# Values' products of four steps in one block of TensorE's queue, four banks for the exponentials, and one product of the first attention moved from GpSimd to ScalarE

## What is computed

```python
# 1. attention of 16 heads of 16 columns in bf16, over a reshaped qkv
xs = conv3(x); xs = xs + xs @ pe_w.T
q, k, v = split(xs @ qkv_w.T).astype(bfloat16)
attn = softmax(q @ k.T / sqrt(16)); o = attn @ v
x = layernorm(x + o @ out_w.T)
# 2. in fp32, 16 heads: masked self attention plus attention over the context
y  = softmax(causal(q @ k.T * scale)) @ v        # 512 x 512 scores, 4 tiles of keys
y += softmax(qc @ kc.T * scale) @ vc             # 512 x 1024 scores, 8 tiles of keys
x = layernorm(x + y @ Wp + bp)
# 3. routed feed forward: argmax over 8 clusters, then over 8 tiles, a small table per token
x = layernorm(x + ffn(x))
```

## Time and profile before

| | us |
|---|---|
| median of three runs | 3291.19 |
| the profiled execution | 3298.75 |
| its span, first to last instruction | 3296.8 |
| TensorE matmul busy | 2772.2 (84%) |
| VectorE busy | 1921.9 (58%) |
| ScalarE busy | 1342.1 (41%) |
| GpSimd busy | 386.0 (12%) |
| mean granted TensorE clock | 0.820 of full speed |

### The profile page before, as it was taken

One profiled execution on the slowest core, in us unless ns is written; L12 is line 12 of the kernel. 1 busy time (PEld: TensorE's weight loads), 2 busy tenths in 40 slices (PEclk: granted clock), 3 DMA queues, 4 the chain that ended last, 5 costly groups with the idle time before them and its releaser, 6 DMA issues.

```text
span 3296.8 us, 46102 instructions
## 1 busy us (share of the span) xinstructions
PE 2772.2 (84%) x12994; PEld 1096.7 (33%) x12994; DVE 1921.9 (58%) x5166; ACT 1342.1 (41%) x2880; POOL 386.0 (12%) x473
## 2 busy tenths in 40 slices
PE   6899858997689977899778997789977899688995
PEld 1343313433134331443314433144331433324322
DVE  7576275753857538564385743856438564486633
ACT  3345243452524525255252552525525154262541
POOL 3100121001200003000030000300003000130000
PEclk7899858999589975899758997589975899758986
DMA  5300032000410004100051000510005000050000
GB/s 133 59 1 1 1 77 52 1 1 1 93 36 1 1 1 100 29 1 1 0 102 28 1 1 0 104 25 1 1 1 109 20 1 1 1 115 1 1 1 7
DMA packets 284202, 91.83 MB, mean 28 GB/s; under 512 B 269344, under 2 KB 279712, under 8 KB 283936
## 3 DMA queue, kind: packets, MB, share of 16 engines
q1 hardware_dynamic: 283936, 88.60, 13.3%
HBM read 17.27 MB, written 4.19 MB: 7 GB/s over the span
## 4 chain that ended last, share of the span: by engine, by line
PE 69%; DVE 14%; ACT 6%; issue 5%; DMA 3%; POOL 2%; DVEq 0%; POOLq 0%; SPq 0%; ACTq 0%
PE bank L1090 16%; PE bank L908 13%; PE bank L1106 11%; PE bank L1056 9%; PE bank L1086 6%; DVE work L592 5%; PE bank L1052 4%; DMA work<-work 3%; ACT work L497 3%; PE bank L1010 2%; ACT work L462 1%; POOL work L426 1%; PE bank L1002 1%; PE bank L1067 1%; PE bank L1114 1%
## 5 line engine op out<-in xcount | busy, mean ns | idle before, releaser
L497 ACT ACTIVATE work<-bank 128x512 f32<-128x512 f32 (+3 forms) x1536 | 754.2, 544 | 892.9 <-PE bank L1090 603.8
L1090 PE MATMUL bank<-q_c,k_c 32*128 32x512 f32 x2048 | 731.7, 669 | 61.8 <-ACT work L497 61.8
L690 DVE TENSOR_REDUCE top_half<-bank 128x1 f32<-128x512 f32 x1024 | 635.4, 683 | 192.9 <-PE bank L1056 192.6
L1056 PE MATMUL bank<-k_c,q_c 32*128 32x512 f32 x2048 | 499.9, 635 | 6.1 <-DVE top_half L690 6.1
L462 ACT ACTIVATE work<-work,neg 128x512 bf16<-128x512 bf16 x512 | 362.8, 709 | 236.9 <-DVE work L592 126.0
L948 PE MATMUL bank<-k,q 32*128 32x512 bf16 x512 | 280.1, 609 | 180.4 <-DVE work L592 145.1
L1106 PE MATMUL bank<-work,v_flat 128*32 128x512 f32 (+3 forms) x3072 | 385.8, 580 | 0.0
L1090 PEld LDWEIGHTS bank<-q_c,k_c 32*128 32x128 f32 x2048 | 226.4, 193 | 357.7 <-ACT work L497 265.4
L592 DVE TENSOR_SCALAR_CACHE_REDUCE work<-bank 128x512 bf16<-128x512 f32 x512 | 321.5, 680 | 34.5 <-issue 31.5
L686 DVE CUSTOM_DVE_ANT_0 masked<-bank,mask_w 128x384 bf16<-128x384 f32 (+3 forms) x512 | 231.3, 489 | 146.3 <-PE bank L1052 141.9
L1086 PE MATMUL bank<-q_s,k_s 32*128 32x512 f32 (+3 forms) x1024 | 268.3, 500 | 19.1 <-ACT work L497 16.7
(11 more groups left out here) (172 smaller groups left out, 2370.9 us busy)
## 6 DMA issues: line engine op xcount, KB each, us to landing
xT_pad<-xT SPq DMA_DIRECT2D x16, 256.0 KB, 4.2
ctx_sb<-ctxT SPq DMA_DIRECT2D x8, 512.0 KB, 3.3
x_res<-x SPq DMA_DIRECT2D x8, 512.0 KB, 5.1
out<-y_sb SPq DMA_DIRECT2D x8, 512.0 KB, 4.5
work<-work SPq DMA_TRANSPOSE x128, 4.3
qk_sb<-qkT SPq DMA_DIRECT2D x1, 512.0 KB, 4.9
...
```

What stands on the lines that cost most here:

```text
L497: nc.scalar.activation(pT[:, k % PT_SLOTS, g, q0:S], bank[:, RING + n % EXP_RING, 0:S - q0], ACT.Exp, scale=SCALE).then_inc(pT_ready, 1)
L690: nc.vector.tensor_reduce(top_half[:, g, t, half:half + 1], scores, AX.X, ALU.max, negate=True).then_inc(slot_out, 1)
L1056: mm(dst, q_c[rows, i, P * t:P * (t + 1)], k_c[rows, i, S * half:S * (half + 1)], start=True, stop=True, tile_position=(GW * g, 0)).then_i ...
L1090: mm(dst, k_c[rows, i, P * t:P * (t + 1)], q_c[rows, i, :], start=True, stop=True, tile_position=(GW * g, 0)).then_inc(sT_mm, 1)
```

## The change

Three things change.

- **The values' products** of four steps are issued together (`BURST`), after the scores of steps 4, 8 and, for the last four steps of a group, step 0 of the next group or the end of the loop. Each such block writes a slot of VectorE's ring of banks 0 to 3, not bank 7. VectorE copies it out of PSUM (`outputs`): the block of self attention and the first of cross attention as a plain copy, the second of cross attention by adding to what was copied. ScalarE's `o_copy` is gone. pT has six slots of a step.
- **Bank 7** goes to the exponentials: `EXP_RING` is 4, in the loop and for the projections (`unit`), and unit 3 waits for the values that stood in bank 7.
- **The first attention**: ScalarE multiplies the fourth tile of every head, after the exponentials of the next head, with an activation Copy with a scale per row. GpSimd does none. VectorE does three tiles of head 15 too. e1 and p1T have four slots.

The lines that only rename semaphores or lay out the slots in `work` are left out:

```diff
     ALL_STEPS = HG * STEPS
-    RING, EXP_RING = 4, 3
+    RING, EXP_RING = 4, 4
+    BURST = 4
+    BURSTS = STEPS // BURST
...
-    A1_BANKS, E1_SLOTS = 6, 3
-    USES = ALL_SCORES + 4 * HG + EXTRAS
+    A1_BANKS, E1_SLOTS = 6, 4
+    USES = ALL_SCORES + (4 + BURSTS) * HG + EXTRAS
     UNITS, CTX_UNITS = 3 * HG, 2 * HG
-    PT_SLOTS = 4
+    PT_SLOTS = 6
...
                     order += [("max", m) for m in range(score_of(i, u, 0), score_of(i, u + 1, 0)) if m < ALL_SCORES]
+                    if burst_at(i, u):
+                        order.append(("pv",) + burst_at(i, u))
                     if u == 3:
...
                                   9: [("qk", 2), ("qk", 3)], 10: [("v", 0), ("v", 1)]}.get(u, [])
-            order.append(("o", CROSS, HG - 1))
+            order += [("pv", HG - 1, BURSTS - 1), ("o", CROSS, HG - 1)]
             assert len(order) == USES - (EXTRAS if last else 0)
...
+        def burst_at(i, u):
+            k = STEPS * i + u
+            return divmod(k // BURST - 1, BURSTS) if k % BURST == 0 and k > 0 else None
...
-                sp.wait_ge(p1_dve, b * P1_DVE + DVE_TILES * (h + 1) + (NT - DVE_TILES) * (h == H - 1))
+                sp.wait_ge(p1_dve, (b * H + h + 1) * DVE_TILES)
                 own_wait(nc.sync)
-                if h < H - 1:
-                    sp.wait_ge(p1_pool, (b * (H - 1) + h + 1) * (NT - DVE_TILES))
-                    own_wait(nc.sync)
+                sp.wait_ge(p1_act, (b * H + h + 1) * (NT - DVE_TILES))
+                own_wait(nc.sync)
                 if h >= E1_SLOTS:
...
-                def norm1(h):
-                    pool.wait_ge(rden_ready, b * H + h + 1)
-                    own_wait(nc.gpsimd)
-                    for t in range(DVE_TILES, NT):
-                        e = e1[:, h % E1_SLOTS, t, :]
-                        nc.gpsimd.tensor_scalar(e, e, rden1[:, h % 2, t:t + 1], None, ALU.mult).then_inc(p1_pool, 1)
-                for h in range(H - 1):
-                    norm1(h)
-                    if h == 11:
-                        pool.wait_ge(o1_copied, b * KD + 1)
-                        own_wait(nc.gpsimd)
-                        nc.gpsimd.tensor_copy(featA[:, 0, :].rearrange("p (r c) -> p r c", c=CHUNKS),
-                                              o1T[:, 0, :].rearrange("p (c r) -> p r c", c=CHUNKS)).then_inc(tok_ready, 1)
+                pool.wait_ge(o1_copied, b * KD + 1)
+                own_wait(nc.gpsimd)
+                nc.gpsimd.tensor_copy(featA[:, 0, :].rearrange("p (r c) -> p r c", c=CHUNKS),
+                                      o1T[:, 0, :].rearrange("p (c r) -> p r c", c=CHUNKS)).then_inc(tok_ready, 1)
                 rstd(0)
...
+                def norm1(h):
+                    act.wait_ge(rden_ready, b * H + h + 1)
+                    for t in range(DVE_TILES, NT):
+                        e = e1[:, h % E1_SLOTS, t, :]
+                        nc.scalar.activation(e, e, ACT.Copy, scale=rden1[:, h % 2, t:t + 1]).then_inc(p1_act, 1)
                 def out1(k):
...
                     if k >= PT_SLOTS:
-                        act.wait_ge(pv_done, b * ALL_STEPS + k - PT_SLOTS + 1)
+                        act.wait_ge(slot_in, base + uses[("pv",) + divmod((k - PT_SLOTS) // BURST, BURSTS)] + 1)
                     q0 = P * u if u < NT else 0
...
-                def o_copy(kind, i):
-                    act.wait_ge(pv_done, b * ALL_STEPS + STEPS * i + (NT if kind == SELF else STEPS))
-                    nc.scalar.copy(o_rows[:, kind, :], bank[:, 7, :]).then_inc(o_copied, 1)
                 for h in range(H):
                     exp1(h)
+                    if h >= 1:
+                        norm1(h - 1)
                     if h == 11:
                         out1(0)
+                norm1(H - 1)
                 context_keys()
...
                         probabilities(i, u)
-                        if u == 1 and i > 0:
-                            o_copy(CROSS, i - 1)
-                        if u == 5:
-                            o_copy(SELF, i)
-                o_copy(CROSS, HG - 1)
...
                     if h >= 2:
-                        dve.wait_ge(p1_pool, (b * (H - 1) + h - 1) * (NT - DVE_TILES))
+                        dve.wait_ge(p1_act, (b * H + h - 1) * (NT - DVE_TILES))
                     nc.vector.reciprocal(rden1[:, h % 2, :], denb1[:, h % 2, :]).then_inc(rden_ready, 1)
...
                     dve.wait_ge(rden_ready, b * H + h + 1)
-                    for t in range(DVE_TILES if h < H - 1 else NT):
+                    for t in range(DVE_TILES):
                         e = e1[:, h % E1_SLOTS, t, :]
...
                                             ALU.min).then_inc(cross_top, 1)
+                def outputs(i, q):
+                    use, n = uses["pv", i, q], BURSTS * i + q
+                    kind = SELF if q == 0 else CROSS
+                    dve.wait_ge(slot_in, base + use + 1)
+                    if q < 2:
+                        nc.vector.tensor_copy(o_rows[:, kind, :], slot(use)).then_inc(slot_out, 1)
+                    else:
+                        dve.wait_ge(slot_out, base + uses["pv", i, q - 1] + 1)
+                        nc.vector.tensor_tensor(o_rows[:, kind, :], slot(use), o_rows[:, kind, :], ALU.add).then_inc(slot_out, 1)
...
                                 maxima(score_of(i, u, g))
+                        if burst_at(i, u):
+                            outputs(*burst_at(i, u))
                         if u == 3 and i < HG - 1:
...
                                 first_v(base, uses)
+                outputs(HG - 1, BURSTS - 1)
                 finish(CROSS, HG - 1)
...
                     i, w = u // 3, unit_w[u % 3]
-                    if u >= 3:
-                        pe.wait_ge(pj_evac, b * UNITS + u - 2)
+                    if u >= EXP_RING:
+                        pe.wait_ge(pj_evac, b * UNITS + u - EXP_RING + 1)
+                    if u == 3:
+                        pe.wait_ge(vj_evac, (b + 1) * PAIRS)
                     project(bank[:, RING + u % EXP_RING, :], lambda k: w[:, k, P * i:P * (i + 1)], lambda k: featB[:, k, :]).then_inc(pj_mm, 1)
...
-                def pv(i, u):
-                    k = STEPS * i + u
-                    pe.wait_ge(pT_ready, b * ALL_SCORES + GH * (k + 1))
-                    if u < NT:
-                        pe.wait_ge(causal_done, b * HG * NT + NT * i + u + 1)
-                    if u == 0 and i > 0:
-                        pe.wait_ge(o_copied, b * 2 * HG + 2 * i)
-                    if u == NT:
-                        pe.wait_ge(o_copied, b * 2 * HG + 2 * i + 1)
-                    q0 = P * u if u < NT else 0
-                    for g in range(GH):
-                        at = u * H * (HD + 1) + (GH * i + g) * (HD + 1)
-                        last = mm(bank[GW * g:GW * (g + 1), 7, q0:S], v_flat[:, at:at + GW], pT[:, k % PT_SLOTS, g, q0:S],
-                                  start=(u in (0, NT)), stop=(u in (NT - 1, STEPS - 1)), tile_position=(0, GW * g))
-                    last.then_inc(pv_done, 1)
+                def pv(i, q):
+                    k = STEPS * i + BURST * q
+                    pe.wait_ge(pT_ready, b * ALL_SCORES + GH * (k + BURST))
+                    if q == 0:
+                        pe.wait_ge(causal_done, b * HG * NT + NT * (i + 1))
+                    dst = free_slot(base, uses["pv", i, q])
+                    for u in range(BURST * q, BURST * (q + 1)):
+                        q0 = P * u if u < NT else 0
+                        for g in range(GH):
+                            at = u * H * (HD + 1) + (GH * i + g) * (HD + 1)
+                            last = mm(dst[GW * g:GW * (g + 1), q0:S], v_flat[:, at:at + GW], pT[:, (STEPS * i + u) % PT_SLOTS, g, q0:S],
+                                      start=(u % BURST == 0), stop=(u % BURST == BURST - 1), tile_position=(0, GW * g))
+                    last.then_inc(slot_in, 1)
...
                 def o_transpose(kind, i):
-                    pe.wait_ge(o_copied, b * 2 * HG + 2 * i + kind + 1)
+                    pe.wait_ge(slot_out, base + uses["pv", i, 2 * kind] + 1)
                     dst = free_slot(base, uses["o", kind, i])
...
                             scoresT(i, u, g)
-                        if u > 1:
-                            pv(i, u - 2)
-                        elif i > 0:
-                            pv(i - 1, STEPS - 2 + u)
+                        if burst_at(i, u):
+                            pv(*burst_at(i, u))
                         if u == 3 and i < HG - 1:
...
                                 first_v(base, uses)
-                pv(HG - 1, STEPS - 2)
-                pv(HG - 1, STEPS - 1)
+                pv(HG - 1, BURSTS - 1)
                 o_transpose(CROSS, HG - 1)
```

11 lines of the change are left out of this document (5 added, 6 removed).

## The result

The changed kernel takes 2972.77 us (median of 4 runs, 2968.98 to 2974.19) against 3292.53 (4 runs, 3290.33 to 3295.98): a ratio of 0.9026, 95% interval 0.9011 to 0.9042.

A forecast was written before the change was run, and what follows sets the result against it. VectorE bounds the first attention, a chain through a bank on TensorE's queue the loop. Gains of 6.0 and 29.5 us a batch, less 6.0 friction, make 233 over eight; plus 20 for the clock, 253: 3038 us, range 2985 to 3185.

The forecast's parts named there:

- The signs that were named: Both stages: three tiles in 0.87, heads every 3.7; 32 product instructions in 3.6, VectorE's idle in one 3 us piece.
- Rival A: Main loop: VectorE takes over more than counted, maxima and TensorE wait behind late copies; time 3147; chance 0.2.
- B: Group 3 of the loop: the clock falls in all of it; time about 3240; chance 0.13.
- C: Groups 0 to 2: half clock where TensorE waits for VectorE's maxima, so slower; time 3351; chance 0.06.
- D: First attention: no gain, since ScalarE or TensorE is as slow as VectorE was; time 3086; chance 0.1.
- I take off 0.5 us for each of 12 blocks, 6.0: Main loop: friction, a block's hand-overs (a semaphore, a refill of two rings), deducted from each batch's gain of 35.1 us.
- The loop without friction: Main loop: gains by blocks of steps sum to 29.5 us a batch before any deduction for hand-overs.
- the terms for steps 1 to 4 of group 3: Group 3 without maxima: narrow tiles, block 2.3 and projection 3.7, written as 11.6 us against 15.8 before; gain 4.2.
- eight gains: Main loop: the gains of 1.6, 0.65 and 1, put at 7.1 us a batch, lost if VectorE takes over.
- The clock: Group 3, steps 5 to 8: half of the half-clock loss returns, 5 us in four of eight batches, 20 us.
- The term per head: First attention: without GpSimd's hold on VectorE a head takes 3.72 us, not 4.16; 14 x 0.43 = 6.0 us a batch.
- a wait that VectorE did not feel: First attention: the fourth slot ends the exponentials' wait for a slot, 0.88 us, said not to affect VectorE.

The follow-up runs named there:

- The copy done twice: Changed kernel with VectorE's copy of a block's sum done twice in each group's first two blocks, 64 copies of 0.69 us more: 2977.29 us, ratio 0.9070.
- one bank less: Changed kernel with three banks instead of four for the exponentials (EXP_RING 3), one bank unused: 3219.46 us, ratio 0.9781.
- blocks of one: Changed kernel with each step's products issued by themselves (BURST 1, 12 a group) instead of four steps' together: 2923.52 us, ratio 0.8905.
- blocks of two: Changed kernel with products issued two steps at a time (BURST 2, six a group) instead of four: 2977.09 us, ratio 0.9069.
- VectorE's four tiles: Kernel before the change with all four tiles of the first attention's products on VectorE, none on GpSimd, three slots: 3256.79 us, ratio 0.9903.

## Why the prediction was wrong

1. **Direction and mechanism: right.** The signs that were named are there: three tiles in 0.88, 32 instructions in 3.64, VectorE's idle time in one piece, steps 5 to 8 well below 15.5. Rival A did not happen: a copy ends 0.33 us before the first maximum. The copy done twice shows that this is all the cover there was. B and C did not happen in the changed kernel, and B did with one bank less. GpSimd is busy 192 us less (190 forecast). What the prediction does not divide is the loop's gain between its two causes: the bank carries it, and the blocks of four are not needed once the bank is there (by the runs with three banks and with blocks of one). D did not happen, though only just: ScalarE is busy 3.5 of a head's 3.65 us.

2. **The step that failed: "I take off 0.5 us for each of 12 blocks, 6.0".** The blocks took what the arithmetic without it said (13.8 for 13.9, 13.35 for 13.4, a mean of 12.5 for 12.5, and group 3 of batch 0, where the clock stood at 1.00, 43.7 for 43.7), and nothing is left over for 0.5 each. The terms that I summed were measured from the start of one operation to the start of another in the earlier trace rows (1.16 to the first maximum, 1.05 for the last tile), so the hand-overs were in them already, and I charged them twice: 48 us of the 77 between 253 and the profiled 330. What a further block does cost is 0.22 us by blocks of two, 0.2 of it in the products' own time. The same margin closed the range too early: the prediction had 2970 without friction and with the clock back, and took 2985 as the lower end; 2972.77 was measured.

3. **The loop without friction: right.** Fastest batch against fastest batch it went from 195.9 to 166.4, 29.5 us; the sum was 29.5 as well. The parts agree within 0.4 us each, but for one with 0.6, which is more than luck; that the sum agrees to the tenth is luck (the first steps of batch 0 took 0.8 us longer than those of the later batches, and the terms for steps 1 to 4 of group 3 add up to 11.4, not to the 11.6 that I wrote; the measured part is 11.8). In rival A, which speaks of eight gains, 7.1 is the sum of six. Windows of the loop in batches 1 and 7 of the kernel before, then batches 0, 1 and 7 of the changed kernel:

```profile
594.76:790.65 195.89, 185.06 (x1133) 70.78 (x1133) 105.29 (x226) 98.61 (x200) 10.26 (x16) 0.99 0.00 1
3032.30:3235.87 203.57, 191.41 (x1093) 66.40 (x1092) 90.56 (x204) 98.63 (x200) 10.17 (x16) 0.87 0.00 1
```

```profile
179.75:346.16 166.41, 161.96 (x1134) 79.77 (x1133) 111.86 (x238) 92.64 (x192) 10.59 (x16) 0.99 0.01 1
543.31:714.79 171.48, 167.02 (x1134) 80.86 (x1133) 111.78 (x238) 92.89 (x192) 10.59 (x16) 0.95 0.01 1
2751.50:2907.21 155.71, 151.61 (x1094) 68.58 (x1093) 96.85 (x216) 91.60 (x192) 10.16 (x16) 0.97 0.00 1
```

4. **The clock: 20 predicted, 30 by what is left** (265.7 less 8 x 29.5). It is not spread as I thought. In batches 0 to 6 the kernel before lost 42 us against its fastest batch and the changed one still loses 31, 5 in each of six batches; the last batch, which ran at 0.87 before and at 0.97 now, gave 18 more than its 29.5. The rows that I read of steps 5 to 8 of group 3 at 0.52 were one of several places, and the falls there did not go away: they became shorter and moved.

5. **Where the gain of the arithmetic was eaten within a batch:** in group 3. The parts there took 1.8, 2.5 and 1.5 us more than at full clock, and all 5.8 us are missing in batch 0, where the clock does not fall (group 3 takes 44.55 us for 50.36). So it is the clock. What brings it down is shown in part. Filling the gap ahead of step 6 kept the clock up behind it in all seven batches of the loop, and closing the gap of 2.2 us ahead of the last block did so for that block. But the first fall, around step 4, came with the gap before it filled, and batch 0 has all three gaps and no fall. So the last two gaps are a condition of the falls behind them, and not the only one; what else decides is open.

6. **First attention: 62 for 48.** The term per head was 0.43 and came as 0.51 (4.16 to 3.65). Two steps in it were off, though they moved the sum little: the fourth slot, which I called a wait that VectorE did not feel, is needed as soon as ScalarE has the product (4.03 a head without it; the whole gain hangs on it), and the Copy took 0.71, at the bound. 12.3 of the 62.4 us are none of the heads': in batches 1 to 7 the second head's scores start sooner, as in all kernels that ran with a changed program. VectorE at the turn of the batch, the kernel before and then the changed one:

```profile
452.82 0.69 DVE L592 TENSOR_SCALAR_CACHE_REDUCE work<-bank 128x512 bf16<-128x512 f32 x1 [5.38 <-issue]
```

```profile
407.12 0.69 DVE L588 TENSOR_SCALAR_CACHE_REDUCE work<-bank 128x512 bf16<-128x512 f32 x1 [3.33 <-issue]
```

Without these 12.3 us the stage gave 50. That this is near the 48 of the forecast is in part luck: from the second head's scores to the sums of head 15 it gave 59, 7.4 a batch where 6.0 was forecast, and what follows, which I took to keep its length, became 1.2 us a batch longer (39.5 for 38.3). In batch 3 the context's keys start 0.6 us later behind those sums, and a projection (`unit`) takes 3.06 us for 2.27, as it runs longer at the lower clock. Why the idle time at the loop's turn is 2 us shorter stays open: no run here isolates it, and each changed program has it (6.9 to 7.4 us from the first head to the second for 9.1, and 7.8 to 8.5 with VectorE's four tiles).

7. **The sum.** 253 predicted; plus 48 of friction that is not there, 12 for the turn of the batch, 2 for the rest of the first stage, 10 for the clock and 5 outside these stages (the lead lost 1 us less than forecast, the tails and the start are 4 us shorter, for no reason that a run shows) make the 330 of the profiled executions. The medians differ by 320, as the profiled execution lies 7.6 us above its median before and 3.8 below it after.
